# VectorE's expert program written out eight times, and the pieces of the weight split moved within the turns

## The chip, the cores and the metric

The kernel runs on one core of one Trainium2 chip. The metric is the device time of one execution in microseconds (us), lower is better. Five engines work side by side and meet only at semaphores: TensorE (PE, matrix products; its weight loads are PEld), VectorE (DVE), ScalarE (ACT), GpSimd (POOL, which here also issues indirect DMAs) and SyncE (SP, which issues plain DMAs). A name with a q behind it (DVEq) is that engine's sequencer, which handles registers, branches and semaphores.

## The reference, cut to what matters

```python
x = layernorm(x + attention(x))          # 16 x 1024 rows of 256
# mixture of experts, 8 experts, each row goes to its 2 best
h = gelu(xg @ w1[e] + b1[e])             # xg: the rows given to expert e; 256 -> 1024
y = h @ w2[e] + b2[e]                    # 1024 -> 256
out = sum over a row's experts of gate * y
x = layernorm(x + out)
```

All is float32. The kernel gets float32 accuracy from TensorE's faster rounded form (fp32r) by splitting each operand into a high part (the value rounded) and a low part (the value minus the high part) and adding three products: high by high, high by low, low by high.

## The kernel before, in words

A first stage of about 600 us computes attention, the first layer norm and the routing. Its loop over pairs of batches (line 213) is a hardware loop on every engine. It leaves a table of rows for each expert, cut in blocks of 256 rows (BLK), and in `plan` the number of blocks of each expert; in this run an expert has 14 to 20 blocks, 129 in all.

The second stage, the expert part, runs over the 8 experts (here e0 to e7) and, in each, over its blocks. A block is one *turn* of every engine's program. Within it the 1024 hidden columns are cut into 4 units g of 256 (UNITS).

- TensorE: `up(0)` to `up(3)` (line 1367, 12 products each, into `h_ps`), `down(0)`, the transposes of the next block's rows (line 1348, into `tb_ps`), `down(1)` to `down(3)` (line 1383, into `y_ps`). `down(g)` waits for `h_lo` of unit g. `up(0)` waits for `bt_lo` of its block, `down(0)` for `y_raw` of the block before.
- ScalarE, for each unit: the gelu of both halves (line 1193), then the high part `h_hi` (line 1196); after the four units the high part of the next block's rows (`bt_hi`) and a copy of these rows.
- VectorE, in `body`: `add_up` (the gated sum with what is in `out`), `base_of`, `spread` (mean and variance), then for each unit `h_lo` (line 1292). After unit 0 come `factors` and `finish_rows` (the layer norm's last step, writing `y`), after unit 3 `split_lo` (`bt_lo`, line 1221), `pick` and `gates` for the next blocks. At the end it waits for TensorE's `y_ps` and adds the bias: `y_raw<-y_ps,b_sb`, line 1316, once per block. Here this instruction is called the *add*, and a turn is measured from one add to the next. In the second turn of an expert (`late`, turn 1) `add_up`, `base_of` and `spread` come after unit 1, `factors` and `finish_rows` after unit 2.
- GpSimd: gathers the rows of the block after next, takes the reciprocal root, gathers `base` from `out`, and puts `y` into `out`.
- SyncE: loads the raw weights of the next expert into `w_raw` once the last split has left it.

The next expert's weights (4096 columns) are also split on VectorE into `w_hi` and `w_lo` of the other buffer, in 8 pieces of 512 columns, each a copy (line 1309) and a subtraction (line 1311). TensorE waits for all 8 before the next expert begins. They lie in the first four turns of each expert but the last, which VectorE's program has written out; the further turns are a hardware loop (line 1325) without pieces. In turn 0 there is a piece after the `h_lo` of each of the units 1, 2 and 3 (that of unit 3 behind `gates`), in turn 1 none, in turn 2 again after the units 1, 2 and 3, in turn 3 after the units 2 and 3.

VectorE's program for the experts is a hardware loop over `half` (line 1328) whose body holds two experts (`eu` 0 and 1); it is run three times, for e0 to e5. e6 and e7 are written out behind it, since e7 splits nothing. So a branch back to the top of this loop is taken twice: from e1 to e2 and from e3 to e4. The other engines' loops over the experts have no part written out.

Of the kernel before, what the change touches and what calls it, by code (L numbers as in the profile page):

```python
# [6 lines left out]
def build(nc, x, x_t, wq, wk, wv_t, wo, wo_t, bo, bo_t, wr_t, w1, b1_t, w2, b2, out):  # L7
    F = mybir.dt.float32
    R = mybir.dt.float32r
    I = mybir.dt.int32  # L10
    ALU = mybir.AluOpType
# [4 lines left out]
    E, _, FF = w1.shape  # L16
# [32 lines left out]
    with outer:  # L49
        def sem(name):  # L50
            return outer.enter_context(nc.semaphore(name))
# [6 lines left out]
        def wait_apart(eng, which, value):  # L58


            eng.wait_ge(which, value)
            eng.sem_inc(apart, 1)


        def keep(name, shape, dt=F):
            return outer.enter_context(nc.sbuf_tensor(name, shape, dt))

        ident = keep("ident", [P, P])
        w_raw = keep("w_raw", [P, 2 * DK * FF])
        w_hi = [keep("w_hi0", [P, 2 * DK * FF], R), None]  # L70
        w_lo = [keep("w_lo0", [P, 2 * DK * FF], R), None]
# [5 lines left out]
        w_loaded = sem("w_loaded")  # L77
        w_split = sem("w_split")
# [9 lines left out]
        with ExitStack() as phase:  # L88
            def sb(name, shape, dt=F):
                return phase.enter_context(nc.sbuf_tensor(name, shape, dt))  # L90
# [53 lines left out]
            late = sb("late", [P, TILES, E])  # L144
# [849 lines left out]
        with ExitStack() as phase:  # L994
# [71 lines left out]
            def column(n, w):  # L1066
                return table[:, bass.ds(n * BT, BT), w]
# [145 lines left out]
            @block_b.vector  # L1213
            def _(dve):
                V = nc.vector
                V.memset(base[:, :, :], 0.0)
                V.memset(y_raw[:, :, :], 0.0).then_inc(y_raw_done, 1)

                def split_lo(n):
                    dve.wait_ge(bt_hi_done, n + 1)  # L1220
                    V.tensor_tensor(xt_lo[:, :, :].rearrange("p k n -> p (k n)"), t_ps[:, :],
                                    xt_hi[:, :, :].rearrange("p k n -> p (k n)").bitcast(F), ALU.subtract).then_inc(bt_lo_done, 1)

                def pick(n):

                    V.tensor_copy(pick_idx[:, :], column(n + 1, 0)).then_inc(pick_ready, 1)

                def gates(n):
                    V.tensor_copy(gate[:, :, :], table[:, bass.ds(n * BT, BT), 2:4].bitcast(F)).then_inc(gate_ready, 1)
                    dve.wait_ge(gate_ready, n + 1)  # L1230
                    V.tensor_scalar(part[:, :], gate[:, :, 1], -1.0, 1.0, ALU.mult, ALU.add).then_inc(put_ready, 1)

                def add_up(n):
                    dve.wait_ge(y_raw_done, n + 1)
                    dve.wait_ge(put_ready, n + 1)
                    if not (isinstance(n, int) and n == 0):
                        dve.wait_ge(base_loaded, 16 * BT * n)
                    for t in range(BT):
                        ins = V.scalar_tensor_tensor(y_raw[:, t, :], y_raw[:, t, :], gate[:, t, 0:1], base[:, t, :],  # L1239
                                                     ALU.mult, ALU.add)  # L1240
                    ins.then_inc(sum_step, 1)

                def base_of(n):

                    V.tensor_copy(base_idx[:, :], column(n + 1, 1)).then_inc(base_ready, 1)

                def spread(n):
                    dve.wait_ge(sum_step, STEPS * n + 1)
                    for t in range(BT):
                        ins = V.bn_stats(stats[:, t, :], y_raw[:, t, :])  # L1250
                    ins.then_inc(sum_step, 1)
                    wait_apart(dve, sum_step, STEPS * n + 2)
                    for t in range(BT):
                        ins = V.bn_aggr(mean_var[:, t, :], stats[:, t, :])
                    ins.then_inc(sum_step, 1)
                    dve.wait_ge(sum_step, STEPS * n + 3)
                    V.tensor_scalar(rstd[:, :], mean_var[:, :, 1], EPS, None, ALU.add).then_inc(var_done, 1)  # L1257
                    V.tensor_tensor(mean[:, :], mean_var[:, :, 0], gate[:, :, 1], ALU.mult).then_inc(sum_step, 1)

                def factors(n):  # L1260

                    dve.wait_ge(root_done, n + 1)
                    V.tensor_tensor(rstd[:, :], rstd[:, :], gate[:, :, 1], ALU.mult).then_inc(sum_step, 1)
                    dve.wait_ge(sum_step, STEPS * n + 5)
                    V.tensor_tensor(rstd[:, :], rstd[:, :], part[:, :], ALU.add).then_inc(sum_step, 1)

                def finish_rows(n):
                    dve.wait_ge(sum_step, STEPS * n + 6)
                    wait_apart(dve, put_done, 16 * BT * n + 16)
                    V.tensor_copy(put_idx[:, :], column(n, 0))  # L1270
                    for t in range(BT):
                        ins = V.tensor_scalar(y[:, t, :], y_raw[:, t, :], mean[:, t:t + 1], rstd[:, t:t + 1], ALU.subtract, ALU.mult)  # L1272
                    ins.then_inc(y_done, 1)

                split_lo(0)
                dve.wait_ge(b2_loaded, 16)
                dve.wait_ge(table_padded, 9 + E - 1)
                pick(1)
                gates(0)

                CH = 2 * DK * FF // 8

                def body(n, e, eu, turn=None, split=False):

                    late = turn == 1
                    if not late:
                        add_up(n)
                        base_of(n)
                        spread(n)
                    for g in range(UNITS):  # L1290
                        dve.wait_ge(h_hi_done, n * UNITS + g + 1)
                        V.tensor_tensor(h_lo[:, g, :], h_ps[:, g, :], h_hi[:, g, :].bitcast(F), ALU.subtract).then_inc(h_lo_done, 1)  # L1292
                        if late and g == 1:
                            add_up(n)
                            base_of(n)
                            spread(n)
                        if g == (2 if late else 0):
                            factors(n)
                            finish_rows(n)
                        if g == UNITS - 1:  # L1300
                            split_lo(n + 1)
                            pick(n + 2)
                            gates(n + 1)
                        if split and turn != 1 and (g >= 1 if turn != 3 else g >= 2):

                            piece = {0: 0, 2: 3, 3: 6}[turn] + g - (1 if turn != 3 else 2)
                            cols = slice(piece * CH, (piece + 1) * CH)
                            dve.wait_ge(w_loaded, 32 * (e + 2))
                            V.tensor_copy(w_hi[1 - eu][:, cols], w_raw[:, cols]).then_inc(w_split, 1)  # L1309
                            dve.wait_ge(w_split, 3 + e * 16 + piece * 2)  # L1310
                            V.tensor_tensor(w_lo[1 - eu][:, cols], w_raw[:, cols], w_hi[1 - eu][:, cols].bitcast(F),
                                            ALU.subtract).then_inc(w_split, 1)

                    dve.wait_ge(y_done, n + 1)
                    wait_apart(dve, h_used, (n + 1) * UNITS)
                    V.tensor_tensor(y_raw[:, :, :], y_ps[:, :, :],  # L1316
                                    b2_sb[:, bass.ds(e * D, D)].rearrange("p (a d) -> p a d", a=1).broadcast_to([P, BT, D]),
                                    ALU.add).then_inc(y_raw_done, 1)

                def expert(half, eu, last):  # L1320
                    e = half * 2 + eu
                    blocks, before = blocks_of(dve, e)
                    for turn in range(4):
                        body(before + turn, e, eu, turn, not last)
                    with dve.Fori(4, blocks) as block:
                        body(before + block, e, eu)

                with dve.Fori(0, E // 2 - 1) as half:
                    for eu in range(2):
                        expert(half, eu, False)  # L1330
                expert(E // 2 - 1, 0, False)
                expert(E // 2 - 1, 1, True)
                total = all_blocks(dve)
                add_up(total)
                spread(total)
                factors(total)
                finish_rows(total)
# [91 lines left out]
```

## Time and profile before

| what | us |
|---|---|
| median of 3 runs (lowest to highest) | 2128.93 (2125.66 to 2129.43) |
| the profiled execution | 2128.42 |
| its span, first to last instruction | 2126.7 |
| TensorE products busy | 2012.0 (95%) |
| VectorE busy | 1484.2 (70%) |
| ScalarE busy | 1228.6 (58%) |
| GpSimd busy | 1258.0 (59%) |
| expert part, in the span | 604 to 2126.7 |

The profile is of one execution. Busy times are those of instructions that do work; registers, branches and semaphore waits are not counted. "Idle before" an instruction is put down to what released it last; "issue" is time in which nothing that the profile shows was waited for. The granted clock is a share of TensorE's full speed.

### The profile page before, as it was taken

The numbers are of one execution on the slowest core, as the hardware profiler recorded it, in microseconds if no ns is written. First come the engines' busy times: TensorE is split into PE (matmuls) and PEld (weight loads), VectorE is DVE, ScalarE is ACT, GpSimd is POOL, SyncE is SP. The second block draws the span as 40 slices with busy tenths as digits, with TensorE's granted clock in tenths as the row PEclk, the third lists the DMA queues.
The fourth block names the chain that finished last, engine by engine and source line by source line (L and its number), as shares of the span: only waits on it lengthen the run. The fifth ranks groups of instructions, "written<-read, shape, count | busy, mean of one in ns | idle before, by whom it ended". The sixth has DMA issues, their size and how long they took to land.

```text
span 2126.7 us, 51586 instructions
## 1 busy us (share of the span) xinstructions
PE 2012.0 (95%) x16208; PEld 1954.1 (92%) x16209; DVE 1484.2 (70%) x4388; ACT 1228.6 (58%) x2775; POOL 1258.0 (59%) x1336
## 2 busy tenths in 40 slices
PE   6999999998269999999999999999999999999997
PEld 5988888887169999999999999999999999999997
DVE  3777887877447667667667767676677676666666
ACT  3566666666345656555656566555556565655654
POOL 1277667776745556565555565466565555655655
PEclk9999999999579999999999999999999999999999
DMA  5234334332222112111211211131131212211221
GB/s 184 80 131 147 126 130 149 121 124 101 71 97 89 42 41 90 50 51 38 89 55 47 96 54 53 47 103 57 53 103 60 65 58 67 66 61 62 74 69 58
DMA packets 102434, 173.11 MB, mean 81 GB/s; under 512 B 26499, under 2 KB 70622, under 8 KB 102256
## 3 DMA queue, kind: packets, MB, share of 16 engines
q0 software_dynamic: 45584, 84.59, 13.0%
q1 hardware_dynamic: 56800, 88.00, 12.1%
q14 instruction: 38, 0.31, 0.1%
q8 instruction: 12, 0.20, 0.0%
HBM read 121.41 MB, written 69.21 MB: 90 GB/s over the span
## 4 chain that ended last, share of the span: by engine, by line
PE 59%; issue 6%; POOL 3%; DVE 2%; DMA 1%; DVEq 1%; POOLq 0%
PE y_ps L1383 29%; PE h_ps L1367 27%; PE tb_ps L1348 2%; POOL rows L1099 1%; DMA out<-y,put_idx 1%; POOL base L1112 1%; POOL rstd_b L1105 1%; POOL out L1120 1%; DVE h_lo L1292 0%; DVE y_raw L1239 0%; DVE y L1272 0%; DVEq L1047 0%; DVEq L1048 0%; DVE w_hi L1309 0%; DVE stats_b L1250 0%
## 5 line engine op out<-in xcount | busy, mean ns | idle before, releaser
L1193 ACT ACTIVATE h_ps<-h_ps,b_sb 128x256 f32<-128x256 f32 x1032 | 415.8, 445 | 595.3 <-PE h_ps L1367 595.3
L1383 PE MATMUL y_ps<-w_hi,h_hi 128*128 128x256 f32 x2064 | 590.0, 286 | 8.5 <-DVE h_lo L1292 8.1
L1367 PE MATMUL h_ps<-bt_hi,w_hi 128*128 128x256 f32 x2064 | 573.4, 278 | 3.4 <-issue 2.0
L1383 PE MATMUL y_ps<-w_hi,h_lo 128*128 128x256 f32 x2064 | 575.9, 279 | 0.0
L1383 PE MATMUL y_ps<-w_lo,h_hi 128*128 128x256 f32 x2064 | 575.4, 279 | 0.0
L1367 PE MATMUL h_ps<-bt_lo,w_hi 128*128 128x256 f32 x2064 | 572.1, 277 | 0.0
L1367 PE MATMUL h_ps<-bt_hi,w_lo 128*128 128x256 f32 x2064 | 571.9, 277 | 0.0
L1383 PEld LDWEIGHTS y_ps<-w_hi,h_hi 128*128 128x128 f32 x2064 | 389.9, 189 | 14.8 <-DVE h_lo L1292 14.5
L1367 PEld LDWEIGHTS h_ps<-bt_hi,w_hi 128*128 128x128 f32 x2064 | 389.2, 189 | 5.2 <-issue 3.4
L1292 DVE TENSOR_TENSOR h_lo<-h_ps,h_hi 128x512 fp32r<-128x512 f32 x516 | 344.6, 682 | 66.8 <-ACT h_hi L1196 66.7
L1383 PEld LDWEIGHTS y_ps<-w_hi,h_lo 128*128 128x128 f32 x2064 | 389.3, 189 | 0.0
L1367 PEld LDWEIGHTS h_ps<-bt_lo,w_hi 128*128 128x128 f32 x2064 | 388.6, 188 | 0.0
L1367 PEld LDWEIGHTS h_ps<-bt_hi,w_lo 128*128 128x128 f32 x2064 | 388.6, 188 | 0.0
L1383 PEld LDWEIGHTS y_ps<-w_lo,h_hi 128*128 128x128 f32 x2064 | 388.3, 188 | 0.0
L381 POOL DMA_INDIRECT slot_table<-entry,where x256 | 280.4, 1095 | 142.4 <-issue 61.1
L1112 POOL DMA_INDIRECT base<-out,base_idx x258 | 269.2, 1043 | 101.1 <-issue 78.5
L1120 POOL DMA_INDIRECT out<-y,put_idx x260 | 266.5, 1025 | 102.4 <-issue 78.5
L1099 POOL DMA_INDIRECT rows<-x_rows,pick_idx x258 | 260.3, 1009 | 101.9 <-issue 82.4
L1196 ACT ACTIVATE h_hi<-h_ps 128x512 fp32r<-128x512 f32 x516 | 308.9, 599 | 16.4
L1105 POOL TENSOR_TENSOR rstd_b<-rstd_b,minus_half_b 128x2 f32<-128x2 f32 x130 | 93.8, 722 | 324.4 <-DVE rstd_b L1257 324.3
L1316 DVE TENSOR_TENSOR y_raw<-y_ps,b_sb 128x512 f32<-128x512 f32 x129 | 89.2, 692 | 241.5 <-PE y_ps L1383 241.5
L1239 DVE SCALAR_TENSOR_TENSOR y_raw<-y_raw,gate,base 128x256 f32<-128x256 f32 x260 | 114.7, 482 | 35.1 <-issue 19.4
(211 smaller groups left out, 3404.9 us busy)
## 6 DMA issues: line engine op xcount, KB each, us to landing
xt_raw<-in_x_t SPq DMA_DIRECT2D x32, 512.0 KB
x_raw<-in_x SPq DMA_DIRECT2D x64, 256.0 KB, 3.2
w_raw<-in_w SPq DMA_DIRECT2D x16, 1024.0 KB
x_rows<-x_sb SPq DMA_DIRECT2D x32, 512.0 KB
out<-alone SPq DMA_DIRECT2D x32, 512.0 KB
rows<-x_rows,pick_idx POOLq DMA_INDIRECT x260
out<-y,put_idx POOLq DMA_INDIRECT x260, 2.5
base<-out,base_idx POOLq DMA_INDIRECT x258
```

Of the source, the lines that this page charges most:

```text
L381: pool.indirect_dma_start(out=table_dram, out_offset=bass.IndirectOffsetOnAxis(ap=where[u][:, c, t:t + 1], axis=0), in_=entry[u][:, c, t, ...
L1099: pool.indirect_dma_start(out=rows[:, t, :], out_offset=None, in_=x1_dram, in_offset=bass.IndirectOffsetOnAxis(ap=pick_idx[:, t:t + 1], ax ...
L1105: G.tensor_tensor(rstd[:, :], rstd[:, :], minus_half[:, :], ALU.pow).then_inc(root_done, 1)
L1112: pool.indirect_dma_start(out=base[:, t, :], out_offset=None, in_=out_dram, in_offset=bass.IndirectOffsetOnAxis(ap=base_idx[:, t:t + 1], a ...
L1120: pool.indirect_dma_start(out=out_dram, out_offset=bass.IndirectOffsetOnAxis(ap=put_idx[:, t:t + 1], axis=0), in_=y[:, t, :], in_offset=No ...
L1193: nc.scalar.activation(half, half, ACT.Gelu_apprx_tanh, bias=b1_sb[:, bass.ds(e * FT + 2 * g + i, 1)]).then_inc(gelu_done, 1)
L1196: nc.scalar.activation(h_hi[:, g, :], h_ps[:, g, :], ACT.Copy).then_inc(h_hi_done, 1)
L1239: ins = V.scalar_tensor_tensor(y_raw[:, t, :], y_raw[:, t, :], gate[:, t, 0:1], base[:, t, :], ALU.mult, ALU.add)
L1292: V.tensor_tensor(h_lo[:, g, :], h_ps[:, g, :], h_hi[:, g, :].bitcast(F), ALU.subtract).then_inc(h_lo_done, 1)
L1316: V.tensor_tensor(y_raw[:, :, :], y_ps[:, :, :], b2_sb[:, bass.ds(e * D, D)].rearrange("p (a d) -> p a d", a=1).broadcast_to([P, BT, D]), ...
L1367: ins = nc.tensor.matmul(h_ps[:, g, (f % 2) * BLK:(f % 2 + 1) * BLK], w[:, c:c + P], v[:, k, :], start=(i == 0), stop=(i == 3 * DK - 1))
L1383: ins = nc.tensor.matmul(y_ps[:, t, :], v[:, g, h:h + P], w[:, c:c + D], start=(f == 0 and t == 0 and part == 0), stop=(f == FT - 1 and t ...
```

## The change

Two things change, both on VectorE alone. The loop over `half` goes: the program of an expert is written eight times, one behind the other, with the expert's number a constant. The loop over an expert's further blocks stays. And each piece of the split gets another place: two in each of the turns 0 to 3. In the turns 0, 2 and 3 one stands between the last unit's `h_lo` and `split_lo`, the other behind `gates`. In turn 1 one stands at the very start, before the first `h_lo`, the other behind `gates`. The instructions of a piece and what they wait for are the same.

```diff
+                def split_piece(e, eu, piece):
+                    cols = slice(piece * CH, (piece + 1) * CH)
+                    dve.wait_ge(w_loaded, 32 * (e + 2))
+                    V.tensor_copy(w_hi[1 - eu][:, cols], w_raw[:, cols]).then_inc(w_split, 1)
+                    dve.wait_ge(w_split, 3 + e * 16 + piece * 2)
+                    V.tensor_tensor(w_lo[1 - eu][:, cols], w_raw[:, cols], w_hi[1 - eu][:, cols].bitcast(F),
+                                    ALU.subtract).then_inc(w_split, 1)
...
                     late = turn == 1
+                    if split and late:
+                        split_piece(e, eu, 2)
                     if not late:
                         add_up(n)
...
                         if g == UNITS - 1:
+                            if split and not late:
+                                split_piece(e, eu, 2 * turn)
                             split_lo(n + 1)
                             pick(n + 2)
                             gates(n + 1)
-                        if split and turn != 1 and (g >= 1 if turn != 3 else g >= 2):
-                            piece = {0: 0, 2: 3, 3: 6}[turn] + g - (1 if turn != 3 else 2)
-                            ... (the same copy and subtraction)
+                            if split:
+                                split_piece(e, eu, 2 * turn + 1)
...
-                with dve.Fori(0, E // 2 - 1) as half:
-                    for eu in range(2):
-                        expert(half, eu, False)
-                expert(E // 2 - 1, 0, False)
-                expert(E // 2 - 1, 1, True)
+                for e in range(E):
+                    expert(e // 2, e % 2, e == E - 1)
```

## Rows read from the trace of the kernel before

**Rows 1.** The page: busy us, share of the span, instructions of each engine.
```profile
PE 2012.0 (95%) x16208; PEld 1954.1 (92%) x16209; DVE 1484.2 (70%) x4388; ACT 1228.6 (58%) x2775; POOL 1258.0 (59%) x1336
```
**Rows 2.** Waits: who waited for whom, us in total, times, longest us.
```profile
PEld y_ps L1383 <- DVE h_lo L1292: 14.5, 31, 3.6
```
**Rows 3.** The chain that ended last, e1 to e2: start us, us, what.
```profile
955.78 3.35 issue
959.13 0.08 DVEq L1328
...
960.57 1.08 issue
```
**Rows 4.** DMA queue of instructions, 955.8 to 964 us: packets, MB, share.
```profile
q14 instruction: 3, 0.02, 1.1%
```
**Rows 5.** All DMA queues from 227 to 417 us, in the first stage.
```profile
q1 hardware_dynamic: 16231, 25.08, 39.1%
q0 software_dynamic: 3072, 0.20, 1.5%
```
**Rows 6.** Windows of the turns 0 to 2, e1, e2, e3, e4, e6, e7.
```profile
core 0: us, PE busy (x) PEld busy (x) DVE busy (x) ACT busy (x) POOL busy (x), PEclk, DMA share, GB/s
769.84:807.02 37.18, 35.74 (x304) 35.13 (x305) 28.45 (x81) 20.81 (x45) 19.52 (x21) 1.00 0.13 40
955.45:998.59 43.14, 39.08 (x303) 38.28 (x304) 28.54 (x81) 20.99 (x45) 20.26 (x21) 0.92 0.12 37
1136.80:1174.01 37.21, 36.64 (x304) 35.30 (x305) 28.70 (x82) 20.74 (x45) 20.08 (x21) 1.00 0.15 48
1356.62:1397.13 40.51, 36.97 (x304) 35.46 (x305) 28.54 (x81) 20.77 (x45) 20.05 (x21) 1.00 0.17 50
...
1709.74:1746.79 37.05, 36.62 (x303) 35.51 (x304) 28.53 (x82) 20.77 (x45) 20.00 (x21) 1.00 0.19 59
1942.60:1978.25 35.65, 35.55 (x303) 35.22 (x304) 22.67 (x69) 20.81 (x45) 19.93 (x22) 1.00 0.21 65
```
**Rows 7.** Windows: turn 0 of e2; one pair of batches; 964 to 971 us.
```profile
955.45:974.22 18.77, 15.06 (x104) 14.87 (x105) 10.34 (x29) 7.05 (x15) 5.43 (x6) 0.82 0.08 23
...
227.00:290.40 63.40, 62.40 (x413) 56.71 (x412) 50.30 (x156) 41.81 (x104) 45.86 (x49) 1.00 0.40 131
964.00:971.00 7.00, 6.11 (x29) 6.12 (x30) 6.36 (x17) 4.53 (x10) 2.94 (x3) 0.51 0.05 17
```
**Rows 8.** The chain in the further turns of e3, then of e4, two turns each.
```profile
1253.83 5.44 PE h_ps L1367 x48
...
1276.64 5.44 PE h_ps L1367 x48
...
1454.66 5.46 PE h_ps L1367 x48
...
1477.66 5.46 PE h_ps L1367 x48
```
**Rows 9.** VectorE's timeline, e3, the add into turn 2, then turn 2: start us, us.
```profile
1161.45 0.69 DVE L1316 TENSOR_TENSOR y_raw<-y_ps,b_sb 128x512 f32<-128x512 f32 x1 [0.91 <-PE y_ps L1383]
...
1168.21 0.62 DVE L1309 CAST w_hi<-w_raw 128x512 fp32r<-128x512 f32 x1
1168.87 0.69 DVE L1311 TENSOR_TENSOR w_lo<-w_raw,w_hi 128x512 fp32r<-128x512 f32 x1
1169.48 0.68 DVE L1292 TENSOR_TENSOR h_lo<-h_ps,h_hi 128x512 fp32r<-128x512 f32 x1
...
1172.94 0.42 DVE L1309 CAST w_hi<-w_raw 128x512 fp32r<-128x512 f32 x1
1173.40 0.69 DVE L1311 TENSOR_TENSOR w_lo<-w_raw,w_hi 128x512 fp32r<-128x512 f32 x1
```
**Rows 10.** VectorE's timeline: the first `h_lo` of turn 1 in e4.
```profile
1375.58 0.69 DVE L1292 TENSOR_TENSOR h_lo<-h_ps,h_hi 128x512 fp32r<-128x512 f32 x1 [2.04 <-ACT h_hi L1196]
```
**Rows 11.** Waits of TensorE from 787 to 793 us, turn 0 of e1.
```profile
PE tb_ps L1348 <- DMA rows<-x_rows,pick_idx: 1.4, 1, 1.4
```

More of the change, by code:

```diff
@@ L1303, in body @@
                             gates(n + 1)
-                        if split and turn != 1 and (g >= 1 if turn != 3 else g >= 2):
-                            piece = {0: 0, 2: 3, 3: 6}[turn] + g - (1 if turn != 3 else 2)
[L1307 to L1312, printed above, removed]
+                            if split:
+                                split_piece(e, eu, 2 * turn + 1)
                     dve.wait_ge(y_done, n + 1)
```

## The prediction

> **What bounds the kernel now.** The page first: TensorE is busy 2012.0 us of 2126.7, VectorE 1484.2 [rows 1]. So the end is set by TensorE, and a change on VectorE alone can only matter where TensorE stands still, or runs slowly, for want of something VectorE makes. The waits say how much that is: TensorE's weight loads waited 14.5 us for `h_lo` of VectorE, in 31 pieces, the longest 3.6 us [rows 2]. That is the whole directly visible stake, small beside 2126.7; short gaps and a lowered clock add to it.
>
> Then the chain of waits in order of time, at the beginnings of the experts. From e1 to e2 it leaves TensorE and shows VectorE's sequencer: 3.35 us of issue at the branch of line 1328, and 1.08 us more a little later [rows 3]. In just this time three packets came in on the queue of instructions [rows 4]: the code at the top of the half loop was no longer at hand and was fetched.
>
> The windows turn this into a price. I cut them at the adds, so each holds the turns 0 to 2 of one expert, the same work on TensorE (303 to 305 products) [rows 6]:
>
> - e7, reached by falling through, no pieces: 35.65 us.
> - e6, reached by falling through, with pieces: 37.05.
> - e3, reached by falling through, with pieces: 37.21, and e5 the same within 0.01; e1 37.18.
> - e2, reached by the branch back: 43.14; e4, the other one: 40.51.
>
> A further turn takes 11.41 us in an odd expert (two from 1253.83 to 1276.64) and 11.50 in an even one (two from 1454.66 to 1477.66) [rows 8], so an even expert like e7 would need 35.65 + 3 x 0.09 = 35.92.
>
> **The change, part by part.** *The loop that goes.* e6 is in the old kernel what e2 and e4 become: an even expert with pieces whose VectorE code is reached by falling through and has its number as a constant. So e2 gains 43.14 - 37.05 = 6.09 us and e4 40.51 - 37.05 = 3.46, together 9.55. Two-thirds of e2's 6.09 is VectorE coming late with the first `h_lo`. The rest is the clock: from 964 to 971 us it was granted at 0.51 of full speed, that is at its lower level, 1.2 GHz, and this window begins when TensorE starts again behind its longest standstill [rows 7, 2]. e4 had the late `h_lo` but 1.00 in its window; so I price the dip at 6.09 - 3.46 = 2.63. Both ends for the 9.55: 9.55 if the dip goes with the stall, 6.9 if a dip comes anyway. I take 9.55, since e3, e4, e6 and e7 all read 1.00. Register instructions saved by the constants I take at nothing: they hide behind VectorE's vector instructions.
>
> *The pieces.* In turn 2 of e3 the copy and subtraction after unit 1 stand directly before the next `h_lo`, at 1168.21 and 1168.87, and this `h_lo` starts at 1169.48 with no idle before it: VectorE, not ScalarE, made it late, by 1.27 us, and a second piece does this again to unit 3 [rows 9]. In the new order the `h_lo` of all units go first; what is then behind them is `split_lo`, which only the next block's `up(0)` needs, after three more `down`. In turn 3 of the old kernel one such piece already stood before `h_lo` of unit 3; it moves likewise. So the pieces in the turns 0, 2 and 3 cease to cost TensorE anything, and the three turns should come down to e7's. That is worth 37.21 - 35.65 = 1.56 each in e3 and e5; 37.05 - 35.92 = 1.13 each in e2, e4 and e6 (the first two on top of the 9.55); for e0, whose first turn has no add before it, I estimate 1.1 like the other even ones. In e1 TensorE stood 1.4 us for gathered rows [rows 11], which the change need not remove; of its 37.18 - 35.65 = 1.53 I take 0.1. Sum: 3.12 + 3.39 + 1.1 + 0.1 = 7.7. Both ends: 9.1 if e1's wait goes too, and 0 if what makes these turns long is not the pieces.
>
> *What is added to turn 1.* One piece goes to the start. There VectorE waits 2.04 us for ScalarE's `h_hi` [rows 10]; a piece takes from 1172.94 to 1174.09, 1.15 us [rows 9], so it is covered, with 0.9 to spare. Without that cover `h_lo` of unit 0 would come up to 1.15 us late, but `down(0)` needs it only after the four `up`. The other goes to the end, before the add. There VectorE is idle 0.91 us [rows 9]; a piece starts 0.08 before the last small instruction ends, so it overruns by 1.15 - 0.91 - 0.08 = 0.16. Late is then the add, and behind it all of turn 2 up to `h_lo` of unit 1, where there is no slack I can see. 0.16 x 7 experts = 1.1 us lost. Ends: 0 and 7 x 0.3 = 2.1.
>
> *Other queues.* No instruction that issues a DMA moves. `pick`, which GpSimd's gather waits for, comes one piece earlier in the turns 0 and 2 and behind as many as before in the others. The wait for `w_loaded` comes later in turn 0 than before, so it is easier. The eighth piece ends at the same place, the end of turn 3, so SyncE's next load and TensorE's wait before the next expert do not move. ScalarE and GpSimd get nothing new.
>
> *The sum.* 9.55 + 7.7 - 1.1 = 16.1. Against the profiled execution's own 2128.42 (span 2126.7 and 1.7 around it) that gives 2112.3 (span 2110.6). The median of the runs, 2128.93, is 0.5 above the profiled one: 2112.8, rounded to 2112.5.
>
> **Rivals.** *A loop across a page of code (slower).* Straight code of about twice the old length means that the inner loops of e1 to e7 lie elsewhere relative to the edges at which code is fetched, and one may lie across an edge; if the fetch ahead pushes out the loop's first part, every turn of it pays for a branch back. Price: one branch back cost e4 3.46 us in all. It cannot cost less than the 3.35 + 1.08 = 4.43 of issue [rows 3] minus all of VectorE's idle time in a turn, 11.41 - 22.67 / 3 = 3.85 [rows 6, 8], which is 0.6. With 12 further turns that is 7 to 42 us, and I take the upper end, since e4's row is the thing itself: 2154. At 3.46 a turn it decides from the fifth turn on, where 16.1 is used up. Against it: in the first stage one pair of batches takes VectorE 156 counted instructions in 63.4 us [rows 7], more than twice an expert's inner loop and twice its three turns (x81) [rows 6], and over three such pairs no instruction packet came at all [rows 5]. A loop that long must cross edges too. Chance 0.05.
>
> The Trainium skill ("Runtime: NRT & Kernel Launch", section "Instruction fetch mechanics") says that most engines hold two blocks of 256 instructions, fetched strictly ahead, and that a taken branch to a place outside this window waits for a fetch. That agrees with the stall at line 1328, and it warns of just this rival; by the silence on the queue in the first stage the warning does not bite for a loop of this size.
>
> *The pieces were not the reason (less gained).* The turns keep their length because of `factors` and `finish_rows`; turn 1 of e3, with no piece in it, is also over 11.41. Then 9.55 - 1.1 is left, 2120. For it: that turn 1. Against: e7 has `finish_rows` in the same places and is 1.1 to 1.6 shorter over the three turns. Chance 0.13.
>
> *The clock dips anyway* at some start of an expert: 2112.5 + 2.6 = 2115. Chance 0.09, inside the range.
>
> *The code is late also when falling through (hardly a change).* With code never run before at each expert, each start might pay what e2 paid. e3, e5, e6 and e7 speak against it, e6 and e7 above all, whose code ran for the first time. If e2 and e4 keep their stalls and the pieces give half, 2128.5 - 3 = 2125. Chance 0.05.
>
> **How the numbers follow.** The forecast has 0.68, the rivals 0.05, 0.13, 0.09, 0.05. A measurement of this kernel can tell about 0.2%, 4.3 us, from no change. Faster by more: forecast, clock, most of the pieces rival, 0.88. Within: the late code and a little of the rest, 0.07. Slower: the page edge, 0.05. The range goes down to 9.55 + 9.1 = 18.65 gained, 2110, less the spread of the runs (their lowest is 3.3 under the median), 2108; and up to the pieces rival, 2120, plus 1: 2121. The likeliest case alone is 2109 to 2117.
>
> **What would show it.** In the changed kernel: no run of several us of issue on VectorE at the start of e2 or e4, at most one or two instruction packets there; the granted clock 1.00 from 955 us on; three turns of e2, e3, e4 and e6 each within 0.5 of 36; no `h_lo` that begins directly behind a subtraction of line 1311; VectorE's idle before the add in turn 1 gone; TensorE's waits for `h_lo` down from 14.5 to 5 or less. The prediction is wrong if the further turns of some expert leave 11.41 or 11.50, if instruction packets come during them, or if turn 1 grows by more than 0.5.

## The result and the profile after

The changed kernel takes 2114.91 us (median of 4 runs, 2113.89 to 2116.48) against 2129.18 (2125.66 to 2130.84) of the kernel before: a ratio of 0.9941, 95% interval 0.9930 to 0.9953 (ratios here are those on record, formed over all the runs; that of the two medians alone would be 0.9933). Once more, beside other variants: 2114.57 against 2126.68, 0.9943 (0.9930 to 0.9957). The profiled execution took 2113.89, its span is 2112.1, 14.6 less than before. I had forecast 2112.5 and a span 16.1 shorter.

The page of the changed kernel, busy us by engine, to be held against [rows 1]:

```profile
PE 1998.9 (95%) x16208; PEld 1946.5 (92%) x16209; DVE 1484.4 (70%) x4387; ACT 1230.3 (58%) x2775; POOL 1258.7 (60%) x1336
```

The same products, 13 us less busy, 1.6 of them in the first stage (up to 604 us). Part of the rest is the lower clock of e2's start, which is gone; what else it is I have not separated. VectorE does the same work. TensorE's waits, its weight loads for `h_lo` first, then its products for gathered rows from 604 us on:

```profile
PEld y_ps L1388 <- DVE h_lo L1305: 1.2, 3, 0.5
```
```profile
PE tb_ps L1353 <- DMA rows<-x_rows,pick_idx: 6.1, 11, 1.1
```

The waits for `h_lo`, 14.5 us in 31 pieces in [rows 2], are down to 1.2. (`h_lo` is now line 1305, the add line 1324, the pieces 1287 and 1289.) But a wait that was one of 1.4 us [rows 11] is now eleven, 6.1 us together: TensorE's transposes wait for gathered rows. (The window of [rows 11], 787 to 793 us, lies in turn 1 of e1, not in turn 0 as its heading says.)

The windows of the turns 0 to 2, cut at the adds, for e2 and e3, and turn 4 of e5 behind them (columns as in [rows 6]):

```profile
953.86:989.84 35.98, 35.44 (x303) 35.24 (x304) 28.51 (x82) 20.80 (x45) 20.45 (x21) 1.00 0.15 44
1128.51:1164.78 36.27, 35.17 (x303) 34.98 (x304) 28.62 (x81) 20.89 (x45) 19.78 (x21) 1.00 0.16 49
1558.36:1570.91 12.55, 11.60 (x102) 11.40 (x101) 7.70 (x23) 6.95 (x15) 7.99 (x9) 1.00 0.71 229
```

e2 went from 43.14 to 35.98 and e3 from 37.21 to 36.27; read in the same way, e4 went from 40.51 to 36.10, e6 from 37.05 to 36.20 and e7 from 35.65 to 35.25 [rows 6]. The granted clock of e2 went from 0.92 to 1.00. The last row is the surprise: a further turn of an odd expert, 11.41 before [rows 8], takes 12.55, with the DMA engines busy to 0.71.

To see where the time went I read each turn's length on TensorE, from the first product of its `up(0)` to that of the next turn (the very last turn to its last product), and summed each turn number over the eight experts (us):

| turn | before | changed | difference |
|---|---|---|---|
| 0 | 108.4 | 95.1 | -13.3 |
| 1 | 97.2 | 97.7 | +0.5 |
| 2 | 97.1 | 92.5 | -4.6 |
| 3 | 92.0 | 91.6 | -0.4 |
| 4 | 92.6 | 96.2 | +3.6 |
| 5 and on | 1023.4 | 1022.9 | -0.5 |
| all | 1510.7 | 1496.0 | -14.7 |

The turns 0 to 2 gave 17.4, more than the 16.1 of my sum; turn 4, which no term of it mentions, took 3.6 back. Turn 4 of e0 to e5 takes 12.02 to 12.55 us, where my prediction had named further turns that leave 11.41 or 11.50 as a sign of being wrong.

The chain of waits of the changed kernel, from turn 3 to turn 4 of e5, shows how:

```profile
1556.63 0.09 DVE pick_idx L1226
...
1557.57 1.34 POOL rows L1099
...
1559.22 6.75 DMA rows<-x_rows,pick_idx
```

A piece stands before `split_lo` and so before `pick`; GpSimd's gather waits for `pick`; and the second half of the gather, issued 0.86 us after the add (at 1558.36), lands 6.75 us later, beside 2 MB of weights: these are loaded from the end of turn 3 on, when the last piece has left `w_raw`. TensorE's transposes begin right behind, at 1566.01. VectorE's timeline of this place before the change and after it, the add that begins turn 3 and `pick`; before, GpSimd's second half of the gather too; after, the last `h_lo`:

```profile
1561.01 0.68 DVE L1316 TENSOR_TENSOR y_raw<-y_ps,b_sb 128x512 f32<-128x512 f32 x1
...
1569.90 0.36 DVE L1226 COPY pick_idx<-table 128x2 int32 x1
...
1572.73 0.97 POOL L1099 DMA_INDIRECT rows<-x_rows,pick_idx  x1 [0.30 <-issue]
```
```profile
1546.94 0.69 DVE L1324 TENSOR_TENSOR y_raw<-y_ps,b_sb 128x512 f32<-128x512 f32 x1 [0.16 <-PE y_ps L1388]
...
1554.28 0.69 DVE L1305 TENSOR_TENSOR h_lo<-h_ps,h_hi 128x512 fp32r<-128x512 f32 x1 [0.64 <-ACT h_hi L1196]
...
1556.55 0.16 DVE L1226 COPY pick_idx<-table 128x2 int32 x1
```

The number of pieces ahead of `pick` in turn 3 is one in both. But `pick` comes 1569.90 - 1561.01 = 8.89 us behind the turn's add before, and 1556.55 - 1546.94 = 9.61 after. In all six experts e0 to e5 it is 0.6 to 0.8 us later. The old place, between two `h_lo`, used time in which VectorE now waits for ScalarE, 0.64 us here; the new place has no such time to use.

Is it the meeting with the load that is new? I read when the second half of the gather was issued and when it landed, in us from the add that ends turn 3, and when the load's first packet came, for e0 to e5 (the lowest and the highest of the six):

| kernel | issued | took | landed | first packet of the load | TensorE waited |
|---|---|---|---|---|---|
| before | -0.02 to 0.48 | 6.2 to 6.5 | 6.2 to 6.7 | 0.02 to 0.50 | 0 |
| changed | 0.79 to 0.96 | 6.1 to 6.8 | 6.9 to 7.6 | 0.81 to 0.99 | 0.30 to 0.95 |

It is not. The gather ran beside the load before too, and took as long; but it landed just as TensorE came to its transposes, 6.5 to 6.7 us behind the add, and in e0 to e3 TensorE began them 0.05 us behind the landing, as it does where it waits for it. There was next to nothing to give away (0.2 us in e4, less elsewhere), and the gather now starts 0.4 to 0.8 us later. The load starts later as well, since the last piece now ends closer to the add.

### The profile page after: what moved, and what is told of

Read it like the earlier page. It is cut to its first block, busy times and chain, and to the rows that moved or that the text cites. A ratio compares the mean times of both kernels' runs of the same rounds, so it can differ in the third digit from the quotient of the medians.

```text
span 2112.1 us, 51506 instructions
## 1 busy us (share of the span) xinstructions
PE 1998.9 (95%) x16208; PEld 1946.5 (92%) x16209; DVE 1484.4 (70%) x4387; ACT 1230.3 (58%) x2775; POOL 1258.7 (60%) x1336
## 3 DMA queue, kind: packets, MB, share of 16 engines
q0 software_dynamic: 45584, 84.59, 13.3%
## 4 chain that ended last, share of the span: by engine, by line
PE 58%; issue 4%; DMA 3%; POOL 2%; DVE 2%; ACT 1%; DVEq 1%; POOLq 0%; ACTq 0%
PE y_ps L1388 29%; PE h_ps L1372 27%; DMA rows<-x_rows,pick_idx 2%; PE tb_ps L1353 2%; POOL rows L1099 1%; DMA out<-y,put_idx 1%; ACT h_ps L1193 1%; POOL base L1112 1%; POOL rstd_b L1105 0%; DVE h_lo L1305 0%; DVE y L1272 0%; DVE y_raw L1239 0%; POOL out L1120 0%; ACT h_hi L1196 0%; DVE bt_lo L1221 0%
## 5 line engine op out<-in xcount | busy, mean ns | idle before, releaser
L1196 ACT ACTIVATE h_hi<-h_ps 128x512 fp32r<-128x512 f32 x516 | 309.3, 599 | 16.3
```

The costliest lines, as they stand in the source:

```text
L1196: nc.scalar.activation(h_hi[:, g, :], h_ps[:, g, :], ACT.Copy).then_inc(h_hi_done, 1)
```

## The experiments

Six of the twelve runs fell on two chips on which the kernel before takes 2126 to 2127 us, near the 2129 of the forecast: the two parts apart, three variants and a repetition, told first. The other six fell on two chips on which it takes 2230 to 2232; they come last. A ratio is always to the kernel before on the same chip.

**The loop alone.** The kernel before with the experts written out and the pieces at their old places.

```diff
-                with dve.Fori(0, E // 2 - 1) as half:
-                    for eu in range(2):
-                        expert(half, eu, False)
-                expert(E // 2 - 1, 0, False)
-                expert(E // 2 - 1, 1, True)
+                for e in range(E):
+                    expert(e // 2, e % 2, e == E - 1)
```

> The kernel before with only the loop over half gone, once more, meant for a chip on which the kernel before takes 2127 to 2129 us. Theory: e2's turn 0 falls from 18.1 to 12.1 and e4's from 15.5 to 12.1, the clock stays at 1.00, all else stays: 9.5 us less than before, a ratio of 0.9955. Rival (the pieces carry more of the 14.3 us, the branch less): a ratio of 0.997 or more. Rival (the loop carries all): 0.994.

Measured: 2117.90 against 2126.61, 0.9955 (0.9941 to 0.9969), which is 9.6 us of 2129, with 6.6 and 12.6 as the interval's ends. The forecast's 9.55 lies in its middle, but not all of it is what I had priced. e2's turn 0 is 11.61 on TensorE and e4's 11.84, together 10.2 us less than before. The turn 0 of e1, e3 and e5 fell too, from 12.32 to 12.38 down to 11.76 to 11.81, and that of e6 by 0.26, 1.9 us in all, with every piece at its old place. Behind the add that begins e3, VectorE starts its next work 0.58 us sooner, first before, then with the loop alone:

```profile
1139.08 0.88 DVE L1239 SCALAR_TENSOR_TENSOR y_raw<-y_raw,gate,base 128x256 f32<-128x256 f32 x2 [1.58 <-issue]
```
```profile
1131.33 0.88 DVE L1239 SCALAR_TENSOR_TENSOR y_raw<-y_raw,gate,base 128x256 f32<-128x256 f32 x2 [1.00 <-DVE y_raw L1316]
```

Before, this idle time is 1.55 to 1.60 us in e1, e3, e5 and e6 and 1.00 in e7; with the loop gone it is 1.00 to 1.02 everywhere. Against this gain stand waits for rows, which I had not expected here; the turns 1 and 4 grew by 0.8 and 1.3:

```profile
PE tb_ps L1345 <- DMA rows<-x_rows,pick_idx: 3.4, 6, 1.1
```

**The pieces alone.** The changed kernel with the five lines of the loop put back in place of the two.

> The kernel before with only the pieces moved and the loop over half kept, once more. The changed kernel reads 0.9942 and the loop alone 0.9955, so if the two parts add up this one reads 0.9987, 2.8 us less than before, with e2 at 18 and e4 at 15.5 in turn 0 and TensorE's other waits for h_lo gone. Rival (behind a long turn 0 GpSimd has time, so turn 1 of e2 and e4 has no wait for rows, and the parts do not add up): 0.998 or less. Rival (the moved pieces alone give nothing, their gain all goes into waits for rows): 1.000.

Measured: 2122.45 against 2125.97, 0.9981 (0.9972 to 0.9990): about 4 us, by its middle nearer to the first rival, but the interval holds 0.9987 too. As this rival says, turn 1 of e2 and e4 has no wait for rows here. The two parts alone sum to 0.0045 + 0.0019 = 0.0064, the changed kernel has 0.0058; the difference is within the intervals, but turn 0 shows a real overlap: the loop alone takes 12.5 us off its sum, the pieces alone 3.0, both 13.3. In e1, e3 and e5 either one brings it to 11.7 to 11.9. e2's turn 0 is 16.64, e4's 16.38. Here the clock was lowered at both; 0.86 over 12 us at e2, as at e4:

```profile
960.00:972.00 12.00, 9.18 (x65) 9.18 (x66) 9.60 (x28) 5.65 (x12) 4.68 (x5) 0.86 0.04 13
```

**Pick ahead of the pieces in turn 3.** The changed kernel with one piece of turn 3 moved from before `split_lo` to behind `gates`.

```diff
-                            if split and not late:
+                            if split and not late and turn != 3:
                                 split_piece(e, eu, 2 * turn)
...
                             gates(n + 1)
+                            if split and turn == 3:
+                                split_piece(e, eu, 2 * turn)
                             if split:
                                 split_piece(e, eu, 2 * turn + 1)
```

> The changed kernel with both pieces of turn 3 behind gates, once more, meant for the same kind of chip. Theory: TensorE's waits for rows in turn 4 of e0 to e5 go (12.0 to 12.6 down to 11.4 to 11.6), 3.5 to 4.5 us less than the changed kernel, a ratio to the kernel before of 0.992. Rival (the load of the weights alone is enough): those waits stay, 0.994. Rival (what made this kernel slow on the chip with 2230 us is in it on any chip): further turns of 12.9 us and a ratio over 1.

Measured: 2109.60 against 2126.61, 0.9920 (0.9906 to 0.9934). The theory holds. Turn 4 falls from 96.2 to 91.6 us over the experts, and TensorE's waits for rows from 604 us on from 11 to 4, all in turn 1. GpSimd's timeline in e5 shows the gather right behind the put, with no wait for `pick`; the add that ends turn 3 is at 1554.51:

```profile
1552.56 0.99 POOL L1099 DMA_INDIRECT rows<-x_rows,pick_idx  x1 [0.33 <-issue]
1553.85 0.98 POOL L1099 DMA_INDIRECT rows<-x_rows,pick_idx  x1 [0.30 <-issue]
```

Both halves are issued before the weights begin to load (the load is issued at 1554.75). Over e0 to e5 the second half is issued 0.22 to 0.65 us ahead of the add and lands 2.5 to 6.1 us behind it, before TensorE asks for it. This and the next one are the fastest versions tried.

**Pick ahead of the pieces in all turns.** The same in the turns 0 and 2 too: nothing stands before `split_lo`.

```diff
-                            if split and not late:
-                                split_piece(e, eu, 2 * turn)
...
                             gates(n + 1)
+                            if split and not late:
+                                split_piece(e, eu, 2 * turn)
                             if split:
                                 split_piece(e, eu, 2 * turn + 1)
```

> The changed kernel with both pieces of the turns 0, 2 and 3 behind gates, none before split_lo. Theory: pick comes 1.1 us earlier in the turns 0 and 2 too, but in turn 1 the gather waits for the landing of the put and for base, not for pick, so this adds nothing in turn 1; the waits in turn 4 go as with turn 3 alone: 0.992. Rival (an earlier pick helps turn 1 too): 0.990. Rival (two pieces in a row before the add delay it in turn 0 and 2): 0.993 or more.

Measured: 2109.48 against 2125.97, 0.9920 (0.9907 to 0.9934). The theory holds here too; 0.990 is outside the interval. The turns 0 and 2 neither gain nor lose: their sums are 95.7 and 92.5, against 95.5 and 92.1 with turn 3 alone. Turn 1 is 96.8 against 97.3, too little to tell.

**The gather of turn 1 issued early.** In turn 1 the gather is held up by something else. GpSimd's timeline in the changed kernel, turn 0 and 1 of e3, where TensorE then stood 1.1 us; `base` waits for the landing of the put, and the second half of the rows is issued last:

```profile
1141.42 1.04 POOL L1112 DMA_INDIRECT base<-out,base_idx  x1 [3.17 <-DMA out<-y,put_idx]
...
1145.38 0.96 POOL L1099 DMA_INDIRECT rows<-x_rows,pick_idx  x1 [0.30 <-issue]
```

In turn 0 of an expert GpSimd waits for the landing of its put before it gathers `base`, and the rows come behind that. The edit takes them past it:

```diff
                     put(n)
+                    gather(n + 2)
                     pool.wait_ge(put_done, 16 * BT * (n + 1) + 16)
                     take_up_sums(n)
+                    root(n + 1)
+                    take_up_sums(n + 1)
+                    put(n + 1)
```

with GpSimd's loop over an expert's blocks starting at 2 instead of 1. This `gather` waits for `pick` of turn 0, so what follows it in GpSimd's program waits too.

> The changed kernel with GpSimd's order in turn 0 and 1 changed: the gather of rows that stood at the start of turn 1 is issued in turn 0, before GpSimd waits for the landing of what it put and gathers base. Theory (TensorE's waits for rows in turn 1, 0.5 to 1.4 us in five experts, come of this gather being queued behind the put, its landing and the gather of base): these waits go, 3 to 4 us less than the changed kernel. Rival (base then comes late in turn 1 and delays add_up and with it h_lo of unit 2): turn 1 stays as long or grows, and nothing is gained.

Measured: 2122.57 against 2126.68, 0.9979 (0.9970 to 0.9988), 8 us slower than the changed kernel. The rival holds. The waits for rows in turn 1 are gone (2.5 us left, in turn 4), but VectorE now waits for `base` seven times, and TensorE for VectorE:

```profile
DVE y_raw L1243 <- DMA base<-out,base_idx: 8.7, 7, 2.1
```
```profile
PE y_ps L1392 <- DVE h_lo L1309: 9.8, 14, 1.5
```

Turn 1 grew from 97.9 us over the experts (the changed kernel on the same chip) to 105.7. Of the two orders tried, one leaves the rows late and the other `base`; a third was not tried.

**The changed kernel again**, on the same chip as the last one.

> The changed kernel once more, on another chip and in more rounds. Four of the kernels so far ran on chips on which the kernel before takes 2230 us instead of 2129, with many further turns of 12.9 us instead of 11.4. Theory (the two parts of the change act in the first turns of an expert on any chip): 0.994 of the kernel before again. Rival (where further turns of 12.9 us occur, their number decides and the change moves it): between 0.99 and 1.02, and the number of long turns, not the first four turns of each expert, explains it.

Measured: 0.9943, as told above. The theory holds, on a chip of the first kind. The changed kernel itself never ran on the other kind, so the rival is not tried.

**The chips with 2230 us.** Here the kernel before takes 2232.26 us (21 runs) on one and 2230.08 on another. In the six kernels profiled there the expert part begins 24 to 36 us later in the span, and many further turns take about 12.9 us. Often a stretch of long turns begins or ends in the middle of an expert.

> The kernel before with the loop over half gone and the pieces where they were. My theory (the loop's two branches back cost 6.09 us at e2 and 3.46 at e4, and nothing else hangs on it): 2129.2 - 9.5 = 2119.7 us, no instruction packets beyond one or two at the start of e2 and e4, clock 1.00 there, three turns of e2 and e4 like e6's 37.05. Rival (most of the measured 14.3 us comes from the moved pieces, the branch is partly hidden): 2123 or more. Rival (the whole gain is the loop's): 2115.

Measured: 2219.38, 0.9938 (0.9913 to 0.9962). The same gain within the noise; 9.5 us would be 0.9957, which the interval holds. The granted clock stays at 1.00 there.

> The changed kernel with the loop over half put back (e6 and e7 written out behind it), so only the pieces have moved. If the two parts add up, 14.3 - 9.5 = 4.8 us are left as gain: 2124.4 us, with TensorE's waits for h_lo gone but for two of about 3 us at e2 and e4. Rival (new waits for gathered rows come from the shorter turns 0, which e2 and e4 here don't have): those waits are fewer than the 12 of the changed kernel, and the gain is over 5.5.

Measured: 2236.99, 1.0035 (1.0009 to 1.0060): a loss where the other chips show a gain. 34 of the 97 further turns are over 12.6 us, and the expectation, made for the other kind of chip, is not tested by this time. The clock was lowered at the start of e2 (a standstill of 4.3 us) and not at that of e4 (2.3 us).

> The changed kernel, but in turn 3 both pieces stand behind gates, so that pick, which GpSimd's gather waits for, comes 1.1 us earlier. Theory: the waits of TensorE for gathered rows in turn 4 of e0 to e5 (0.6 to 1.2 us each, some 5 us in all) come of pick being held up by the piece before split_lo in turn 3; they go, 2114.9 - 4.5 = 2110.4 us. Rival (the load of the next raw weights, which starts at the end of turn 3, alone slows the gather): the waits stay at half or more, 2112.5 or more. Rival (the piece behind gates delays the add instead): turn 3 grows and nothing is gained, 2115.

Measured: 2284.96, 1.0242 (1.0221 to 1.0263): one of the two fastest kernels on the first kind of chip is the slowest here, with 67 of the 97 further turns over 12.6 us (30 with the loop alone). None of the three times comes out here, and the trace is nearest to the first rival: three waits for rows in turn 4 stay, 0.45, 0.39 and 1.39 us in e0, e3 and e5, though in e0 and e3 the gather was issued 0.69 us ahead of the add; the theory is borne out by the run above, on the other kind of chip, and not by this one. 26 us among e0's further turns, on this chip and on one of the first kind:

```profile
720.00:746.00 26.00, 24.76 (x204) 23.59 (x203) 14.79 (x46) 13.91 (x30) 13.70 (x15) 1.00 0.13 40
```
```profile
720.00:746.00 26.00, 26.00 (x228) 26.00 (x228) 16.85 (x48) 13.66 (x30) 15.40 (x16) 1.00 0.17 51
```

204 products against 228, at the same granted clock. VectorE waits 4.6 us before such an add, for something that the profile calls remote.

> The changed kernel with the loads of the weights of e1 to e7 cut to 32 columns of the 4096 (the other columns keep the weights of e0); pieces, waits and order are the same. Theory (the gather of turn 4 is late because pick is late and the load of 2 MB of weights runs at the same time; both are needed): the waits for rows in turn 4 vanish, those in turn 1 stay, about 2110 us. Rival (late pick alone): the waits in turn 4 stay at 0.6 to 1.2 us. Rival (both kinds of wait come of the load): those in turn 1 go as well, 2107.

Turn 4 is 94.0 us over the experts, with the load it is 98.4, 98.4, 99.2, 98.3 and 98.7 in the five others on these chips; turn 1 is 98.3, among their 97.2 to 98.7. TensorE has no wait for rows in any turn 4, though the second half of the gather is issued 0.1 to 1.3 us behind the add, as late as with the load: it takes 2.7 to 3.0 us instead of 6.1 to 6.8. The waits in turn 1 stay, 0.5 to 0.9 us in e0 to e3. So the load is needed for the wait in turn 4 and is not what causes that of turn 1. The time of the one run, 2232.49, says nothing in view of the long turns. The kernel leaves out most of the weights, so its output is not that of the reference.

```diff
+            if isinstance(e, int):
                 ... (the two loads of 1 MB as before, for e0)
+            else:
+                for i in range(2):
+                    sp.dma_start(w_raw[:, 16 * i:16 * i + 16], w1[e, 0:P, 16 * i:16 * i + 16]).then_inc(w_loaded, 16)
```

**A standstill at every expert.**

```diff
+                    if e > 0:
+                        for i in range(2):
+                            V.tensor_reduce(spare[:, 2 * e + i:2 * e + i + 1], b2_sb[:, :], X, ALU.add)
```

> The changed kernel with two reductions over 2048 columns, about 2.2 us each, put into VectorE at the start of e1 to e7, before turn 0: the delay of the branch back without the branch, seven times. Theory (a late first h_lo costs TensorE some 3 us of standing still, and now and then a dip of the clock on top of it, 2.6 us): turn 0 of e1 to e7 each 3 to 3.5 us longer, and one or more of the seven 6 us longer, with the granted clock under 1 there. Rival (the dip at e2 had nothing to do with the standstill): all seven read 1.00.

Measured: 2242.90. The two reductions take 4.48 us of VectorE. Turn 0 of e1 to e7 is 17.8, 18.6, 20.0, 14.1, 15.8, 19.9 and 16.3 us on TensorE. 12 us around the standstills of e3 and e4; in the other five windows the clock is 0.72, 0.86, 0.86, 0.73 and 0.86:

```profile
1203.00:1215.00 12.00, 7.89 (x44) 7.69 (x43) 11.14 (x28) 5.65 (x12) 2.75 (x3) 0.72 0.05 18
1429.00:1441.00 12.00, 10.03 (x85) 9.59 (x84) 11.14 (x28) 6.95 (x15) 2.76 (x3) 1.00 0.06 23
```

Six of seven standstills went with the lower clock; only e4's did not, and it is the shortest, in two parts of 1.3 and 1.7 us, where the others are 2.5 to 4.5. The rival is refuted, and the dip is far commoner than the theory had it. The turns are 2.5 to 8.5 us longer than the 11.6 of the changed kernel, more than forecast in most; on this kind of chip turn 0 of e1 to e7 takes up to 14.3 us with no branch back and no reductions, so I take no price from it.

**Code moved against its pages.**

```diff
                 CH = 2 * DK * FF // 8
+                for _ in range(60):
+                    dve.wait_ge(table_padded, 9 + E - 1)
```

> The changed kernel with 60 more wait instructions, all satisfied, ahead of e0 in VectorE's program, where it stands idle for the first rows: every inner loop moves by 60 instructions against the edges of the code pages. Theory (a loop of some 50 instructions across an edge costs nothing, as those of e5 and e6 in the changed kernel show, where the packet falls into the first further turn and none follows): same time as the changed kernel, further turns 11.41 and 11.50. Rival (it costs when the loop lies badly): some expert's further turns are longer throughout, with instruction packets in each of them.

Measured: 2235.83 against 2230.08, in one run each. The time decides nothing: 38 of the 97 further turns are over 12.6 us, but 30 to 67 are in the other kernels on these chips. The packets do. In this kernel's own trace e0 and e7 have an instruction packet in turn 4 and none behind it, and e0's turns behind turn 4 take 11.50 to 11.89; no further turn of any expert has one after turn 4. In the changed kernel the same is seen in e5 and e6. In e5 the packet comes in turn 4, the first run of the inner loop, which I read as an edge of code inside the loop; the queue of instructions from 1558 to 1570 us:

```profile
q14 instruction: 1, 0.01, 0.2%
```

From 1570 us to the end of the expert this queue has none, and the turns 5 to 14 take 11.39 or 11.42. The rival is not seen in any expert.

## Why the prediction was right, and where it was not

The number came out 1.5 us of span from the forecast, and part of that closeness is luck: gains that I had put at nothing and losses that I had not thought of nearly cancel. My own signs of being wrong came in part: turn 4 left 11.41 and 11.50 in six experts, turn 1 of e3 grew by 0.87 us, and an instruction packet fell into a further turn of e5 and of e6, this last at no cost.

**The loop that goes: right for e2 and e4, and a term put at nothing was not.** 9.55 forecast for these two, 9.6 us measured for the loop alone in all. TensorE's turn 0 says 10.2 for e2 and e4, read off the old kernel's own e6, with no model of a fetch. The register instructions, "I take at nothing: they hide behind VectorE's vector instructions", did not hide: at an expert's start VectorE had no vector work to hide them behind, and began 0.55 to 0.6 us later than in e7. Without the loop that is gone, and TensorE's turn 0 is 1.9 us shorter in e1, e3, e5 and e6 together. Whether it was the expert's number in a register or the loop's own branch I cannot say; e6, whose number was a constant already, had it too. New waits for rows, 2.1 us in the turns 1 and 4, hid this gain in the total. Of the packets at e2's start, three in [rows 4], one is left from 953 to 965 us.

**The clock: right in kind; its price and its odds were off.** I priced the dip as 6.09 - 3.46 = 2.63, on one standstill that had it and one that had not. But e2's standstill was also longer, 3.4 us against 2.7, so 0.8 of the 2.63 was no clock at all. And e4's clean one was no rule: with the pieces alone both standstills, 3.2 and 2.9 us, had the dip. The forecast was spared, since both standstills go, and the rival that the clock dips anyway is refuted: it read 1.00 at the start of every expert from e1 on.

**The pieces: right in kind, too large a term.** TensorE's waits for `h_lo` went from 14.5 to 1.2. But 7.7 - 1.1 = 6.6 us were forecast for them, and alone they gave about 4 (0.9981, ends 2.1 and 6.0), and with the loop gone already some 3 more (0.9955 against 0.9941 and 0.9943). I had counted all of the 1.56 us in e3 and e5 as theirs; some 0.6 of it, in turn 0, went with the loop alone too. The rest of the shortfall is waits for rows. e1 gained 1.5 where I had taken 0.1, since its old wait for rows shrank from 1.4 to 0.5.

**The added pieces in turn 1.** The idle time before the add, 0.91 in [rows 9], is 0.02 or less in e0, e1, e2, e5 and e6; in e3 and e4, where TensorE stood for rows in this turn, 0.42 and 0.25 are left. Turn 1 in all grew by 0.5, and its waits for rows alone by 1.5 (1.4 before, 2.8 after), so the term of 1.1 us lost to an overrun is not seen there; I did not measure it by itself.

**The step that failed: "`pick` ... behind as many as before in the others", and "SyncE's next load ... do not move".** I counted pieces ahead of `pick` and took the same number for the same time. In turn 3 `pick` came 0.72 later (e5), the gather with it, and the load, which waits for the last piece, 0.4 to 0.8 us later too. The gather's landing had no time to spare before the change, and I had not looked at that. Cost: 3.6 us in turn 4, in six experts (e6 has no load behind it and no wait). Moving that piece alone took 4.9 us off (0.9943 to 0.9920); the kernel with less of the load shows that the gather is late only when the load runs beside it. The first is shown on one kind of chip and the second on the other. In turn 1 the count itself was wrong: `pick` had no piece ahead of it and has one now, which the cover by ScalarE makes harmless.

**The wait in turn 1.** It was in the trace of before, once [rows 11], and I left it out of e1's gain but did not ask who would be next. With turn 0 0.3 to 0.8 us shorter in e1, e3 and e5 to e7 (and by 4 to 6.5 in e4 and e2), the landing of the put is what the next rows wait for, in up to five experts. This I argue from the timeline, and from the early gather, which removed it and paid more elsewhere.

**The rivals.** A loop across a page of code: e5's and e6's, as I read their packets, are across an edge and pay nothing; nor does e0's in the kernel with 60 more instructions. The pieces were not the reason: refuted by turn 2, whose sum is 97.1 before, 96.7 with the loop alone and 92.5 with both. The late code when falling through: refuted, VectorE's idle time at the start is 1.00 to 1.01 us in every expert from e1 on.

**What stays open.** Why the further turns of some chips take 12.9 us, and why the piece moved in turn 3 goes with more of them. The forecast holds for the chips like the one whose profile I had. I can't say what the changed kernel takes on the others: it was not run there.

## What to carry to other kernels

When a step is moved past another, compare the times at which the next engine's trigger comes, not the number of steps ahead of it: a step that sat in a forced wait was free there. And before you call a transfer undisturbed, look how long before its use it lands: here it was 0.2 us at most, so a trigger 0.7 us later was paid almost in full. Where a kernel already holds one copy of what the change will make of the others, as e6 here, its length is the best forecast there is, but only for what that copy shows free of the loop: e6 still bore the late start, and e7 did not.

## What the hardware showed that I had not expected

- A standstill of TensorE at an expert's start was followed by a granted clock of half for a few us in 10 of the 13 cases in these traces: in all seven longer than 3 us (3.1 to 4.5: e2 before, e2 with the pieces alone on either kind of chip, four with the reductions), and in three of the six of 1.7 to 2.9 us. Those of 2.9, 2.9 and 2.5 had it, those of 2.7, 2.3 and 1.7 had not. One more, of 1.5 us, in turn 2 of e7 with the pieces alone on a chip of the second kind, was followed by it too; others of 1.3 to 1.5 us were not. As an estimate from turn 0's length less 11.6 and less the standstill, such a place cost 1.7 to 4.3 us on top; e4 before, with no dip, 1.3, and e4 with the reductions nothing.
- A branch back over VectorE's two-expert body cost it 3.35 + 1.08 us [rows 3]; VectorE's loop over one expert's further blocks took no packet after its first run, even where I read an edge inside, and its loop over the pairs of batches none from 227 to 417 us [rows 5].
- An indirect gather of 128 rows of 1 KB landed in 6.1 to 6.8 us while 2 MB of weights were loading (turn 4 of e0 to e5, before and changed), in 2.7 to 3.0 us in turn 4 of the kernel with less of the load, and in 2.73 us in turn 1 of e3, where no weights were loading:

```profile
1145.38 2.73 DMA rows<-x_rows,pick_idx
```

- Two of the four chips that the later runs fell on ran the same program 5% slower; in the long turns of the trace shown the granted clock was 1.00 as well. There the order of two variants was reversed.
